# A graph network's third attention layer: the probabilities in PSUM instead of SBUF

## The reference

```python
h = (x @ W_i).reshape(n, H, C)                       # 4 heads of 32
e = leaky_relu(es[src] + ed[dst])                    # a score for each edge and head
m = segment_max(e, dst)
p = exp(e - m[dst])
alpha = p / segment_sum(p, dst)[dst]
out = segment_sum(alpha[:, :, None] * h[src], dst)   # weighed rows, summed by destination
```

## Time and profile before

| what | value |
|---|---|
| median of three runs | 9245.97 us |
| the profiled execution: time, span | 9241.63 us, 9239.8 us |
| TensorE matmul busy | 5626.5 us (61%), 34288 instructions |
| VectorE busy | 5638.8 us (61%), 13019 instructions |
| ScalarE busy | 3271.8 us (35%), 7522 instructions |
| GpSimd busy | 5375.1 us (58%), 5192 instructions |
| gathers, L649 (all layers) | 4992, 5087.9 us busy, 1626.1 us idle before them |
| weighings, L1853 (all layers) | 1248, 841.6 us busy, 695 ns each |
| exponentials, L829 (all layers) | 156, 48.3 us busy, 310 ns each |

### The profile page before, as it was taken

How to read it: one execution, slowest core, us unless ns; L and a number is a source line. 1 busy time by engine, 2 the same in 40 slices (tenths; PEclk the granted TensorE clock), 3 DMA queues, 4 the chain that set the end, 5 groups by cost and what they waited for, 6 DMA issues and landing times.

```text
span 9239.8 us, 129442 instructions
## 1 busy us (share of the span) xinstructions
PE 5626.5 (61%) x34288; PEld 4513.0 (49%) x34288; DVE 5638.8 (61%) x13019; ACT 3271.8 (35%) x7522; POOL 5375.1 (58%) x5192
## 2 busy tenths in 40 slices
PE   4999879964555555555455555555534545445456
PEld 3777646653544445444444444454434444444444
DVE  6888721135666666666466666666645555555555
ACT  3555400023333333333343333333323333333334
POOL 2000100047777777775677777777657777777770
PEclk9999989965555555555555555555555555555558
DMA  3333335404444444443344444444423333233321
GB/s 101 136 139 139 125 140 192 175 16 120 119 119 116 122 113 124 114 116 82 96 113 118 119 116 121 113 123 113 104 65 80 85 80 85 79 85 80 85 79 32
DMA packets 601474, 989.07 MB, mean 107 GB/s; under 512 B 331107, under 2 KB 455044, under 8 KB 561524
## 3 DMA queue, kind: packets, MB, share of 16 engines
q0 software_dynamic: 163760, 357.05, 17.1%
q1 hardware_dynamic: 217540, 544.34, 16.8%
q10 hardware_dynamic: 219648, 81.82, 3.4%
HBM read 758.42 MB, written 224.34 MB: 106 GB/s over the span
## 4 chain that ended last, share of the span: by engine, by line
PE 27%; DVE 22%; DVEq 18%; POOL 14%; issue 13%; DMA 5%; ACT 1%; POOLq 0%; SPq 0%; ACTq 0%
DVEq L1264 15%; PE bank L959 13%; POOL arena L649 13%; DVE acc L1866 10%; DMA arena<-row_table,staged_idx 4%; PE bank L1182 3%; PE bank L984 3%; DVE arena L1853 2%; DVE arena L1822 2%; PE bank L1122 2%; DVEq L1866 2%; DVE x_mem L1535 1%; DVE arena L1815 1%; DVEq L1858 1%; PE bank L1247 1%
## 5 line engine op out<-in xcount | busy, mean ns | idle before, releaser
L649 POOL DMA_INDIRECT arena<-row_table,staged_idx x4992 | 5087.9, 1019 | 1626.1 <-issue 1467.3
L1182 PE MATMUL bank<-arena 128*128 128x136 f32 x9984 | 2487.9, 429 | 1207.5 <-DVE acc L1866 1045.8
L1182 PEld LDWEIGHTS bank<-arena 128*128 128x128 f32 x9984 | 2195.9, 316 | 1372.1 <-issue 1231.0
L1866 DVE TENSOR_TENSOR acc<-acc,bank 128x136 f32 x4992 | 1476.7, 296 | 1020.7 <-issue 798.1
L804 ACT ACTIVATE pick_dist<-col,dst_local 128x128 bf16<-128x128 f32 x4992 | 1523.3, 388 | 1092.0 <-PE bank L1182 1091.3
L959 PE MATMUL bank<-arena 128*128 128x385 bf16 (+1 forms) x7546 | 1342.6, 327 | 49.5 <-DVE arena L1639 33.0
L597 POOL TENSOR_TENSOR arena<-acc,node_stat 128x896 f32 x14 | 24.5, 1748 | 1721.8 <-POOLq L609 956.3
L959 PEld LDWEIGHTS bank<-arena 128*128 128x128 bf16 x7546 | 711.2, 98 | 476.5 <-DVE arena L1639 33.2
L1138 PE MATMUL bank<-ident,arena 128*32 128x128 f32 x624 | 161.5, 414 | 1206.8 <-DVE arena L1785 1206.8
L1853 DVE TENSOR_TENSOR arena<-arena,prob 128x528 f32<-128x528 f32 x1248 | 841.6, 695 | 0.2
L1782 DVE TENSOR_TENSOR arena<-arena 128x128 f32<-128x128 f32 x156 | 60.8, 390 | 1229.2 <-DMA arena<-row_table,staged_idx 1229.2
(11 more groups left out here) (354 smaller groups left out, 5383.0 us busy)
## 6 DMA issues: line engine op xcount, KB each, us to landing
arena<-dst_rows SPq DMA_DIRECT2D x156, 1024.0 KB
cell_rows<-arena SPq DMA_DIRECT2D x76, 1568.0 KB, 5.2
arena<-cell_rows SPq DMA_DIRECT2D x76, 1568.0 KB, 6.5
arena<-row_table,staged_idx POOLq DMA_INDIRECT x4992
edge_stats<-x_mem ACTq DMA_DIRECT2D x416, 192.0 KB, 3.5
x_mem<-in_edge_attr SPq DMA_DIRECT2D x208, 192.0 KB
x_mem<-segment_flags SPq DMA_DIRECT2D x416, 96.0 KB
arena<-change_rows SPq DMA_DIRECT2D x312, 64.0 KB
```

What stands on the lines that cost most here:

```text
L649: pool.indirect_dma_start(gathered[:, at, :], None, table, bass.IndirectOffsetOnAxis(staged_idx[:, at:at + 1], 0)).then_inc(att_gathered[n ...
L1182: mm = pe.matmul(region(k)[:, 0:ROW], pick[:, k, :], gathered[:, b * GROUP + k, :], start=True, stop=True)
L1866: done = dve.tensor_tensor(row, row, region(m * BATCH + k), ALU.add)
```

## The change

In the third layer (n = 2, where no edge statistics are turned) ScalarE writes the probabilities of buffer b into PSUM bank b, columns 0 to 127, and the weighing reads its second input there. The first two layers keep the SBUF tile.

```diff
--- before.py
+++ after.py
@@ -369,6 +369,11 @@
         att_flags = [att.flags0, att.flags1]
         RNG = GROUP // ROUND
         BACK_AT, SCALE_AT, ENDS_AT, CROSS_AT = 0, P, GROUP * PARTS * HEADS, GROUP * PARTS * HEADS + 2 * GROUP
+
+        def prob_of(n, b):
+            if n < STATS_LAYERS:
+                return prob[:, b, :, :]
+            return bank[:, b, 0:HEADS * GROUP].rearrange("p (h s) -> p h s", h=HEADS)
 
         def region(k):
             return bank[:, 4 + k % (2 * BATCH) // 2, k % 2 * ROW:(k % 2 + 1) * ROW]
@@ -826,7 +831,7 @@
 
                 def act_exps(head, b):
                     act.wait_ge(att.shifted, head + 1)
-                    nc.scalar.activation(prob[:, b, :, :], score[:, :, :], ACT.Exp).then_inc(att.prob, 1)
+                    nc.scalar.activation(prob_of(n, b), score[:, :, :], ACT.Exp).then_inc(att.prob, 1)
                     act.wait_ge(att.scale_rows, head + 1)
                     nc.scalar.activation(old_scale[:, :], bank[:, 3, SCALE_AT:SCALE_AT + HEADS], ACT.Exp
                                          ).then_inc(att.scale, 1)
@@ -1851,7 +1856,7 @@
                 def weigh(G, b, m):
                     batch_rows = group_rows(b)[:, m * BATCH:(m + 1) * BATCH, 0:AW].rearrange("p s (h c) -> p s h c", h=HEADS)
                     dve.tensor_tensor(batch_rows, batch_rows,
-                                      prob[:, b, :, m * BATCH:(m + 1) * BATCH].rearrange("p h s -> p s h").unsqueeze(3)
+                                      prob_of(n, b)[:, :, m * BATCH:(m + 1) * BATCH].rearrange("p h s -> p s h").unsqueeze(3)
                                       .to_broadcast([P, BATCH, HEADS, HW]), ALU.mult).then_inc(att.weighted, 1)
 
                 def add_batch(G, slot, m):
```

## The result

| | before | after |
|---|---|---|
| median of 21 runs each | 9245.64 us (9242.1 to 9258.87) | 9228.78 us (9223.57 to 9240.18) |
| ratio, 95% interval | | 0.9983 (0.9976 to 0.9989) |
| profiled execution: time, span | 9241.63, 9239.8 us | 9227.06, 9225.3 us |
| third layer, first gather to end of the last | 2169.1 us | 2151.7 us |

The change takes 16.9 us off the medians; 9228 was forecast. In the profiled executions the third layer is 17.4 us shorter, though the spans differ by 14.5 only: the first layer of the profile after happens to be 3.9 us longer, and it runs the same instructions.

The account below looks back on a forecast made before the run. GpSimd's issue of gathers was taken to bound the third layer. The terms -7.8 - 8.7 - 0.6 - 1.1 = -18.2 us took 9246.0 to 9227.8, say 9228; range of 8 in 10: 9212 to 9246.

Parts of the forecast that it names:

- The bound: Third layer: GpSimd's issue of gathers paces it, so a change is worth what it takes off GpSimd.
- The rule of the hold: VectorE instruction with two SBUF inputs over a gather's early point lengthens it, 234 of 234; one PSUM input, none of 124.
- c, the doubled hold: Ninth gather held twice in 7 groups: freed, each wins a step of 1.25 us, -8.7; one gather 14, -0.6 us.
- a, late weighings: First three weighings of a group, beside gathers 21 to 23: their holds come off whole, -7.8 us.
- b, gather 3: Weighing 4 over gather 3: its 9.0 us of holds costed at nothing, since two later holds cover it.
- d, the weighing: Three weighings per group in VectorE's chain, 7 ns shorter each with a PSUM input: -1.1 us, bounds -2.3 to +15.
- R2: Weighing longer by 50 to 120 ns, so the gain shrinks: 9236 to 9246 us; chance 0.12.
- R3: PSUM operand repeated 33 times streams slowly; slower from 240 ns more per weighing, 9266 us; chance 0.08.
- e, the exponential: ScalarE's exponential writing to PSUM may be shorter or longer; tenths of a us hide in its wait for TensorE.
- R4: Holds come from the weighing's first input or output in SBUF, so they stay: 9246 us; chance 0.05.
- R1: Held gathers slip past their holders, so more comes off: 9219 us, or near 9195; chance 0.13.
- The prediction's own period: GpSimd's period per group: VectorE's chain to the end of the second building of the masks, then 18 free gathers.

Follow-up runs that it names:

- g4_sbuf: The changed kernel with its PSUM write kept and a second exponential to SBUF, which all weighings read: 9240.8 us, 0.9999 of before.
- g1_after: The changed kernel, run again beside the kernel before: 9224.6 us, ratio 0.9983.
- i_all: The changed kernel with probabilities in PSUM in the first two layers too, plus three waits and a moved copy: 9156.8 us, 0.9907 of before.
- g3_inplace: The changed kernel without the copy of the turned scores from PSUM to SBUF, in all three layers: 9260.8 us, 1.0022 of before.
- i_all_inplace: As i_all, with the copy of the turned scores also taken out in all layers: 9205.3 us, 0.9958 of before.
- g2_inplace3: The changed kernel without the copy of the turned scores from PSUM to SBUF, in the third layer only: 9221.1 us, 0.9979 of before.
- f2_late: As g4_sbuf, but weighings 1 to 3 of a third-layer group read PSUM; in a slow session: 10279.0 us, 0.9946 of before.

## Why the prediction was right, point by point

**The bound** (gathers pace the layer, only their busy time counts) holds: busy time fell by 17.5 us and length by 17.4, and again by 14.6 from g4_sbuf to g1_after.

**The rule of the hold** is right but lacks a condition. The prediction says that a VectorE instruction of the kinds it names, if it lies over the point some 0.13 us after a gather's start, always holds the gather, 234 of 234. In the same layer 121 more gathers have such an instruction over the point (83 times a weighing, 36 times L1822) and aren't held; it began between 0.03 us before and 0.11 us after the gather. The earlier trace rows have one: the gather at 8036.74 takes 0.94, though L1822 runs from 8036.81. The prediction used the condition in step c ("ahead of L1822 and passes") without stating it. No term of the sum hangs on the count of 234.

**a, late weighings, -7.8.** Gathers 21 to 23 went from 9.0 to 1.3 us, -7.7. Of the 1.3 left, 1.2 stand under the rescaling L1845 (after's L1850), which reads `old_scale` in SBUF; the step's 7.8 us did not include it. This term was isolated in the trace only, by place.

**b, gather 3, nothing.** -9.0 at gather 3, +8.9 at gather 6; gather 6 at 1.57 (1.5 to 1.6 was said). In the first two layers of i_all the cover is not whole: gather 3 goes from 8.7 to 0 and gather 6 from 22.6 to 28.4 in the first, from 8.8 to 0 and from 22.7 to 26.9 in the second.

**c, the doubled hold, -9.3.** Gathers 9, 12, 13 and 14 together: 48.2 to 39.2 us, -9.0. All 7 ninth gathers are back under 1.5 us, no gather 12 is held, and the long gather 14 (8374.51, 2.16 us) takes 1.52. That a weighing from SBUF is needed for the doubling was an inference from 7 groups; g3_inplace and i_all_inplace show it on 87 and 97, for a scan with L1769 behind it. The size of c, like that of a, is read by place in the trace.

**d, the weighing, -1.1.** The mean fell by 12 ns, not 7 (702 to 690), inside the bounds of -15 and +100; the median by 3 (700 to 697). That the mean came out near the forecast is luck, since the reason was another: more than half of the 12 ns is the eighth weighing of each group, 751 ns on average before and 698 after; before, it mostly began together with a gather (as at 8042.31 above). The three weighings in the chain became 4 ns shorter each, so the term was 3 x 51 x 4 ns = 0.6 us and not 1.1; the chain L1782 to the second L1769 has its median at 16.19 instead of 16.20 us, which agrees. R2 and R3 are out. The Trainium skill ("VectorE: DVE Perf Modes", The TRN2 errata) has 120 cycles for a PSUM source and 58 for SBUF. The 62 cycles between them don't show here, where one input stays in SBUF and the one in PSUM is repeated 33 times.

**e, the exponential.** It became 29 ns shorter (310 to 281), and g4_sbuf, with a second one, costs nothing.

**R4** fell with g4_sbuf, and with it the remark of the Trainium skill ("SBUF — State Buffer", Who interferes with whom) that a `tensor_tensor` was not seen to stall a DMA issued by GpSimd; the page's rule on one or two SBUF inputs agrees with all 2737 cases. **R1** did not come in this kernel, but its mechanism (a gather that slips past its holder) gave 9 us a layer at the statistics scan in i_all, and some 3 to 5 us at gather 6.

The steps failed where I used them on a new edit: for g2_inplace3 I took the chain's end as fixed at L1769 and let it move continuously. The prediction's own period (a chain and 18 free gathers) has a whole number in it, and I didn't ask when it would turn to 19.

## What to carry to other kernels

Where GpSimd issues DMAs one after another, look at each for what VectorE instruction stands over it: one with both inputs in SBUF that is already running when the DMA's instruction starts, and still runs 0.14 us later, holds it to its end; moving one of the inputs to PSUM freed it here. Sum the holds by their place in the period; those with another holder behind them are only moved, those behind the last holder come off whole, and two back to back can cost a step. Before shortening the chain between two releases, count how many free steps fit behind it: what is saved may be handed back as one step more, or put a step under a holder that it missed until then.

## What the runs showed of the hardware

- Whether a held gather gets through between two back-to-back VectorE instructions depends on the operands of a weighing that starts only later. Gather 13 under a scan, with the masks 0.07 us ahead of its end, was let go at the scan's end in all 97 groups with PSUM weighings and held on through the masks in all 87 with SBUF weighings, though weighing 7 starts 0.58 us behind the scan's end (2525.25 and 2524.67). Which of the weighings does it, and how, the runs don't show.
- When a weighing from SBUF and a gather start together, VectorE pays instead of GpSimd. In 51 cases the weighing began up to 0.03 us before the gather; it took 0.74 to 0.77 us instead of 0.70, and the gather its usual 0.94.
- A held gather ends 0.77 us (2521.49 + 1.49 against 2522.21) to 0.82 us (2523.95 + 2.19 against 2525.32) behind its holder's end.
- ScalarE's exponential of 128 x 128 is faster into PSUM (281 ns) than into SBUF (310).
- The same kernel took 9241 to 9247 us in some sessions and 10323 to 10331 in others, with the undisturbed gather at 0.944 to 0.947 us in all, and long stops of GpSimd in the slower ones (312.3 us in f2_late's third layer). One chip number of the record stands for both.
